# A routing search that counts in PSUM: the transposed values are read where TensorE left them

## The reference, cut to what matters

```
cap = ceil(1.25 * 4096 / 16)                       # 320
probs = softmax(x @ Wg)                            # 4096 x 16
top1_val, top1_idx = probs.max(-1), probs.argmax(-1)
masked = where(top1_idx == n, top1_val, -inf)      # for each expert n
vals, idx = top_k(masked, cap)                     # the kept tokens
out = gelu(x[idx] @ W1[n] + b1[n]) @ W2[n] + b2[n] # for each expert
y = x; y[idx] = out                                # other tokens keep x
```

## Time and profile before

| | us |
|---|---|
| median of 3 runs | 1411.47 (1409.69 to 1411.76) |
| profiled execution | 1411.86 |
| its span, first to last instruction | 1410.0 |
| DVE busy | 905.2 (64%) |
| PE busy | 1073.4 (76%) |
| ACT busy | 554.4 (39%) |
| POOL busy | 423.5 (30%) |
| mean granted TensorE clock | 0.818 of full speed |

### The profile page before, as it was taken

How to read it: one execution, slowest core, us unless ns; L and a number is a source line. 1 busy time by engine, 2 the same in 40 slices (tenths; PEclk the granted TensorE clock), 3 DMA queues, 4 the chain that set the end, 5 groups by cost and what they waited for, 6 DMA issues and landing times. The chain is left out here.

```text
span 1410.0 us, 21638 instructions
## 1 busy us (share of the span) xinstructions
PE 1073.4 (76%) x6380; PEld 792.0 (56%) x6382; DVE 905.2 (64%) x3040; ACT 554.4 (39%) x1111; POOL 423.5 (30%) x463
## 2 busy tenths in 40 slices
PE   4788879999995765675478278857999999568842
PEld 1655669899993443632456155535567767445621
DVE  7777755656654888599822677756444445547768
ACT  2476434444443222232023256531334445446531
POOL 1344100000100111061262844401771457324311
PEclk9799969999997555555579569976999999869975
DMA  8344010000002300204032343200337751044202
GB/s 266 92 124 109 7 30 1 1 2 0 1 1 89 91 0 14 84 0 120 13 97 72 88 122 101 72 2 10 96 120 208 216 165 51 13 127 123 72 3 60
DMA packets 108320, 101.05 MB, mean 72 GB/s; under 512 B 10864, under 2 KB 88048, under 8 KB 107824
## 3 DMA queue, kind: packets, MB, share of 16 engines
q1 hardware_dynamic: 76464, 74.22, 18.5%
q0 software_dynamic: 6400, 12.92, 3.5%
q10 hardware_dynamic: 25344, 12.59, 3.1%
HBM read 62.13 MB, written 37.75 MB: 71 GB/s over the span
## 5 line engine op out<-in xcount | busy, mean ns | idle before, releaser
L858 DVE TENSOR_REDUCE mha_nm<-mha_pS 128x16 f32<-128x1024 f32 x96 | 117.2, 1221 | 25.0 <-PE mha_pS L620 24.8
L798 POOL TENSOR_TENSOR mha_ks<-KS,w_ctx 104x1024 fp32r<-104x1024 f32 (+1 forms) x48 | 90.8, 1893 | 94.7 <-POOLq L100 51.5
L1451 ACT ACTIVATE ffn_hid<-ffn_pH,w_ffn 128x512 f32<-128x512 f32 x128 | 85.5, 688 | 55.2 <-PE ffn_pH L1374 54.5
L741 ACT ACTIVATE XH<-mha_pST 128x1024 f32<-128x1024 f32 x96 | 97.8, 1018 | 10.5 <-PE mha_pST L641 10.4
L620 PE MATMUL mha_pS<-mha_ks,mha_qs 96*128 96x256 f32 (+1 forms) x384 | 79.7, 334 | 26.5 <-DVE mha_nm L858 20.0
L1387 PEld LDWEIGHTS ffn_pE<-W2R,ffn_hid 128*128 128x128 f32 x768 | 94.6, 194 | 4.4 <-issue 0.2
L1563 DVE SCALAR_TENSOR_TENSOR ffn_acc<-ffn_pE,ffn_wt,ffn_acc 128x128 f32<-128x128 f32 x192 | 54.0, 345 | 66.7 <-PE ffn_pE L1387 66.7
L1387 PE MATMUL ffn_pE<-W2R,ffn_hid 128*128 128x128 f32 x768 | 95.2, 278 | 0.0
L620 PEld LDWEIGHTS mha_pS<-mha_ks,mha_qs 96*128 96x128 f32 (+1 forms) x384 | 58.8, 212 | 42.0 <-issue 20.5
L2500 POOL DMA_INDIRECT leaf_rows<-XH,tree_place x64 | 63.2, 987 | 57.5 <-DVE tree_place L2580 38.3
L1479 POOL TENSOR_TENSOR X<-X,ffn_xh 128x512 f32<-128x512 f32 (+1 forms) x8 | 10.3, 1284 | 210.9 <-DVE ffn_xh L1509 210.9
(11 more groups left out here) (525 smaller groups left out, 2852.9 us busy)
## 6 DMA issues: line engine op xcount, KB each, us to landing
mha_qs<-queries SPq DMA_DIRECT2D x72, 256.0 KB, 4.0
tree_leaf<-in_leaves_dram SPq DMA_DIRECT2D x96, 96.5 KB
queries<-mha_qh SPq DMA_DIRECT2D x24, 256.0 KB, 2.1
queries<-mha_ql SPq DMA_DIRECT2D x24, 256.0 KB, 2.5
leaf_rows<-top_none SPq DMA_DIRECT2D x12, 512.0 KB, 6.7
tree_xs<-leaf_rows ACTq DMA_DIRECT2D x24, 256.0 KB, 3.2
leaf_results<-tree_ys ACTq DMA_DIRECT2D x24, 256.0 KB
EW<-in_L_W_dram SPq DMA_DIRECT2D x32, 128.0 KB, 2.6
```

The lines of the kernel that those rows point to most:

```text
L741: act.activation(PT[b % PB][:, CU * i:CU * i + CU, :], pST[:], ACT.Exp, scale=SC).then_inc(s["P"], 1)
L798: pool.tensor_tensor(ks[b % KB][0:K1, :, :, :], kb, hb, ALU.mult).then_inc(s["k"], 1)
L858: dve.tensor_reduce(nm[:, t, :], pS[:], AX.X, ALU.max, negate=True).then_inc(s["nm"], 1)
L1451: act.activation(hid[p % 2][:, c, :], pH[c][:], ACT.Gelu, bias=b).then_inc(s["h"], 1)
```

## The change

The tile `MT`, a copy of `pM` in SBUF, goes, and so does the DVE copy that filled it with its wait. The 28 + 1 counts read `pM` itself. `hit` and `ones` move up by a quarter of `found`.

```diff
-        MT, ones, hit = (found[:, T * N1 * n:T * N1 * n + T * N1] for n in range(3))
+        ones, hit = (found[:, T * N1 * n:T * N1 * n + T * N1] for n in range(2))
...
             dve.wait_ge(s["MTp"], 1)
-            link(dve.tensor_copy(MT, pM[:]))
             own0 = link.n

             def count(k, at, op):
-                dve.scalar_tensor_tensor(hit, MT, at, ones, op, ALU.mult, accum_out=cnt[:, 0:1]).then_inc(s["cnt"], 1)
+                dve.scalar_tensor_tensor(hit, pM[:], at, ones, op, ALU.mult, accum_out=cnt[:, 0:1]).then_inc(s["cnt"], 1)
```

## The result

| | before | after |
|---|---|---|
| median of 6 runs, us | 1410.64 (1409.14 to 1414.37) | 1404.10 (1399.95 to 1405.01) |
| ratio after / before | | 0.9947 (0.9930 to 0.9964) |
| profiled execution, us | 1411.86 | 1404.30 |
| span, us | 1410.0 | 1402.4 |

The ratio is 7.5 us (5.1 to 9.9) of 1411, the medians differ by 6.5. The forecast was 1405.8, 5.7 us less than before: the direction and the main mechanism held. The times alone don't prove that, since the interval holds 5.7; the profiles show which parts were missed.

A forecast was written before the change was run, and what follows sets the result against it. VectorE's search was taken as the bound, its counts stalled by GpSimd's SBUF reads. Terms 5.68 + 0 + 0 = 5.7 us off 1411.86 gave 1406.2, and 1405.8 with the median's 0.39; own range 1404.2 to 1407.4, wide range 1403.5 to 1408.7.

The forecast's parts named there:

- DVE is the path of the search, and what it saves arrives: Routing search: VectorE busy 59.38 of 64.00 us, other engines wait for it; its savings start the experts earlier.
- The excess of the counts goes, 5.68: 28 search counts: reading PSUM ends stalls beside GpSimd's reads, 955 to 752 ns each, 5.68 us; bounds 0 to 5.68.
- Undisturbed counts cost the same from PSUM: 29 counts: same form from PSUM takes 746 to 753 ns against 752; taken as 0, bounds -0.17 to +0.29 us.
- The copy is worth 0: Search start: removing the 692 ns copy gains 0, since TensorE's keys hold the first sum; other end 0.73 us.
- POOL at 2.35 or less, no new wait, PE not the limit: Beside the search: GpSimd's 2.79 us operation falls to 2.35, moving `hit` adds no wait, TensorE keeps 0.19 us slack.
- what DVE saves in the search, the experts start earlier: Between search and experts: nothing has a fixed time, so the saving passes on; experts' first transposes 712.8 to 707.1 us.
- a spread of the range: TensorE's granted clock may rise elsewhere once later work moves 5.7 us earlier; counted only within 1404.2 to 1407.4 us.
- stall stays: Counts: output in SBUF or `ones` causes the stall, so it remains; gain 0 to 0.7 us, chance 0.08.
- dearer in PSUM: Counts: a PSUM start-up hidden in other forms costs 0.3 to 1.9 us; 1407.7 us at chance 0.06.
- lost behind: After the search: something that doesn't move holds the experts' start, so the gain is lost; 1411.5 us, chance 0.04.
- slower: Search rounds: counts wait 0.63 us for TensorE's PSUM key writes, 17.0 us in 27 rounds; 1422.8 us, chance 0.04.

The follow-up runs named there:

- e5: Changed kernel with a useless VectorE copy of the PSUM values in each of 27 search rounds; ratio to the kernel before 1.0077 (1.0047 to 1.0107).
- e2: Kernel before, SBUF copy kept, but the tile of ones placed in a PSUM bank; ratio to the kernel before 0.9941 (0.9918 to 0.9964).
- e3: Kernel before with GpSimd's tensor_tensor operations beside the search turned into memsets that only write; ratio to the kernel before 0.9954 (0.9937 to 0.9971).
- e4: Changed kernel with the same GpSimd tensor_tensor operations turned into memsets; ratio to the kernel before 0.9941 (0.9923 to 0.9960).
- e6: Changed kernel, first sum over partitions ahead of one key matmul pair, `low` one round later; ratio to the kernel before 0.9944 (0.9922 to 0.9966).
- e1: Changed kernel with the removed copy put back, counts still reading PSUM; ratio to the kernel before 0.9939 (0.9918 to 0.9959).
- d1: Changed kernel with a useless VectorE copy in eight rounds in the middle of the search; ratio to the kernel before 0.9977 (0.9956 to 0.9998).

## Why the prediction was right or wrong

- *DVE is the path of the search, and what it saves arrives*: right; in e5 19.0 us of search came out as 19.1 of time, within some 5 us.
- *The excess of the counts goes, 5.68*: right, 5.69; e2, e3 and e4 show its cause from three sides.
- *Undisturbed counts cost the same from PSUM*: right, 751 against 752. The overhead of some 125 ns on PSUM against 60 on SBUF that the Trainium skill gives ("Perfetto Trace Analysis", section "Optimizing Scalar/DVE Operations"), 1.9 us by my estimate, doesn't show in this form.
- *The copy is worth 0*: nearly, 0.17 (2.03 against 1.86 to the first `ge`); `low` waited 0.60 for ScalarE as foretold. e6 shows the cover. The pause of 0.22 that goes with its instruction (gone in after, back in e1) was in no term.
- *POOL at 2.35 or less, no new wait, PE not the limit*: right but for 0.02 (2.35 to 2.37; `ge` waited for PE 0.4 in all, as before).
- *The step that failed* is that everything behind the table only moves: "what DVE saves in the search, the experts start earlier", and keep their length. They took 74.3 us instead of 76.0, 1.7 us less, because TensorE's clock rose 23.7 us behind the table instead of 28.4. I had this only as a spread of the range, not as a term, and so put it at nothing in the sum; the copy (0.17) and the pause (0.22) were put at nothing as well. With it the sum is 5.69 + 0.17 + 0.22 + 1.7 = 7.8 against a profile of before that is long (7.5 by the ratio), and about 7.2 against a mean of before's three.
- Rivals: *stall stays* is refuted (no count over 753 beside POOL's reads), *dearer in PSUM* too; *lost behind* is refuted: the experts' first transposes follow the table by 19.3 us as before; *slower*: 749 to 751 while PE writes its banks beside.
- What stays open: the 3.2 us ahead and the 3.3 behind in the first pair of profiles. They change between profiles of one kernel (the part behind the experts, the same code in all, takes from 634.0 us in e5 to 643.9 in e3), so I take them as spread. Whether before is dearer by some 2 us in a part that I don't see, as d1's 3.2 (0.3 to 6.2) hints, was not settled.

## What to carry to other kernels

A DVE operation with both tensors in SBUF that shows now and then twice its duration should be laid beside POOL's operations in order of time: if POOL reads SBUF then, try one input in PSUM. Here that, or POOL only writing, took the whole excess away, and the copy to SBUF that was to save PSUM reads cost 0.37 us and brought nothing, since a count from PSUM took 751 ns against 752. Look at minimum, median and maximum of a line before its mean; the difference times the count is the price. A removed operation at the head of a loop is worth only what the other engines' covers leave, here 0.17 of 0.73. And a saving of a few microseconds can move TensorE's clock rises behind it: a bound of some 2 us either way belongs in the range.

## What the runs showed that I had not expected

- The granted clock's rise in the experts' stage came 23.4 to 24.7 us or 28.4 to 29.4 us behind the table and nowhere between, in 18 profiles, with the stage 74.3 to 74.6 or 76.0 to 76.6 us long; lengthening the search by 2.1, 3.5, 5.6, 7.0, 12.0 and 19.0 us gave long, short, long, short, long, long, and the kernel before, 6.1 longer, gave long twice and short once.
- One DVE instruction more or less ahead of the loop moved or removed an "issue" pause of 0.22 to 0.25 us inside it (rounds counted from 0: before, e1 and e3 in round 19; after, e2 and e4 none; e6 in round 1). Why was not found.
- A tensor_scalar with accumulator on one PSUM input takes the 751 ns of the two-input form.
